# A windowed attention stage: the causal mask written into the score banks by ScalarE, and the value products moved next to the score products

## What is computed

```python
qkv = x @ Wqkv; q, k, v = jnp.split(qkv, 3, -1)          # 16 heads of 64
q = l2norm(q) * qs; k = l2norm(k) * ksc
q = q * cos * scale + rotate_half(q) * sin * scale        # k the same with 1 / scale
# windows of 32 tokens; each window looks at itself and at the one before
bk2, bv2 = (look(bk), look(bv))
mask = (it < jb) | (it > jb + w) | (jb == -1)
sim = jnp.einsum('bhwie,bhwje->bhwij', bq, bk2) * QK_SCALE
sim = jnp.where(mask, -jnp.finfo(sim.dtype).max, sim)
attn = jax.nn.softmax(sim, -1)
out = jnp.einsum('bhwij,bhwje->bhwie', attn, bv2)
x = out @ Wo + x
x = ffn_layer(shift_tokens(x), ...) + x                   # layer norm, W1, gelu gate, W2
```

## Time and profile before

| | before |
|---|---|
| median of three runs | 3678.64 us (3673.33 to 3685.43) |
| span of the profiled execution | 3676.2 us |
| PE busy | 3451.3 us (94%) |
| DVE busy | 2806.8 us (76%) |
| ACT busy | 2365.2 us (64%) |
| POOL busy | 2815.1 us (77%) |
| share of PE in the chain that ended last | 85% |

### The profile page before, as it was taken

How to read it: one execution, slowest core, us unless ns; L and a number is a source line. 1 busy time by engine, 2 the same in 40 slices (tenths; PEclk the granted TensorE clock), 3 DMA queues, 4 the chain that set the end, 5 groups by cost and what they waited for, 6 DMA issues and landing times.

```text
span 3676.2 us, 148973 instructions
## 1 busy us (share of the span) xinstructions
PE 3451.3 (94%) x64612; PEld 2721.5 (74%) x64612; DVE 2806.8 (76%) x4876; ACT 2365.2 (64%) x4307; POOL 2815.1 (77%) x3470
## 2 busy tenths in 40 slices
PE   3799986999999999999999999999999999999997
PEld 2566544788877888777888778877788887788775
DVE  3477666888887888878888878887788888788863
ACT  3333223677766777777777677776677777777663
POOL 1355546998887888878888888888788888888772
PEclk9799997999999999999999999999999999999999
DMA  3333212111111111211111121112111111112110
GB/s 100 98 97 93 87 31 58 47 43 39 46 47 49 40 41 44 51 44 42 45 38 46 44 52 39 42 43 52 40 46 42 40 45 50 44 40 50 36 43 24
DMA packets 126733, 183.48 MB, mean 50 GB/s; under 512 B 29824, under 2 KB 61440, under 8 KB 126080
## 3 DMA queue, kind: packets, MB, share of 16 engines
q1 hardware_dynamic: 119232, 146.15, 15.8%
q0 software_dynamic: 6848, 27.80, 2.5%
HBM read 59.01 MB, written 14.16 MB: 20 GB/s over the span
## 4 chain that ended last, share of the span: by engine, by line
PE 85%; POOL 5%; DVE 3%; issue 3%; ACT 1%; DMA 1%; SPq 0%; ACTq 0%; POOLq 0%; DVEq 0%
PE bank L550 22%; PE bank L622 10%; PE bank L633 9%; PE bank L595 7%; PE bank L560 5%; PE bank L570 4%; PE bank L606 4%; PE bank L696 3%; PE bank L674 3%; PE bank L685 3%; PE bank L582 2%; PE bank L465 1%; PE bank L525 1%; PE bank L642 1%; PE bank L504 1%
## 5 line engine op out<-in xcount | busy, mean ns | idle before, releaser
L550 PE MATMUL bank<-wqkv,xs 128*128 128x512 f32 x3456 | 1061.5, 423 | 17.1 <-DVE m L1029 13.1
L1684 POOL TENSOR_TENSOR m<-m 128x512 f32<-128x512 f32 x576 | 728.7, 1285 | 45.2 <-DVE m L1029 42.6
L550 PEld LDWEIGHTS bank<-wqkv,xs 128*128 128x128 f32 x3456 | 582.8, 191 | 146.0 <-issue 56.9
L1029 DVE TENSOR_TENSOR m<-bank,tab 128x512 f32<-128x512 f32 x768 | 521.5, 679 | 0.7 <-POOL m L1684 0.3
L1358 ACT ACTIVATE sq<-bank 128x512 f32<-128x512 f32 x768 | 458.5, 597 | 98.1 <-PE bank L550 54.2
L1692 POOL TENSOR_TENSOR S<-S,nw 128x1024 f32<-128x1024 f32 x192 | 383.3, 1996 | 168.0 <-DVE S L1060 168.0
L1040 DVE TENSOR_REDUCE ss<-sq 128x8 f32<-128x512 f32 x768 | 504.9, 674 | 0.0
L1700 POOL TENSOR_TENSOR S<-S,rs 128x512 f32<-128x512 f32 x384 | 411.0, 1091 | 69.7 <-DVE rs L1074 67.9
L622 PEld LDWEIGHTS bank<-P,big 64*64 64x64 f32 x24576 | 379.6, 135 | 79.8 <-issue 72.3
L1027 DVE TENSOR_TENSOR m<-bank,tab 128x512 f32<-128x512 f32 x576 | 392.1, 681 | 57.4 <-ACT sq L1358 41.9
L633 PE MATMUL bank<-OT,wo 128*128 128x128 f32 x3072 | 389.9, 282 | 40.8 <-ACT P L1397 27.6
(11 more groups left out here) (232 smaller groups left out, 6457.1 us busy)
## 6 DMA issues: line engine op xcount, KB each, us to landing
big<-vst SPq DMA_DIRECT2D x1536, 64.0 KB
stage<-in_wqkv SPq DMA_DIRECT2D x36, 256.0 KB, 3.0
tab<-in_tab SPq DMA_DIRECT2D x48, 128.0 KB, 2.2
xsort<-big SPq DMA_DIRECT2D x4, 960.0 KB, 8.6
big<-xsort SPq DMA_DIRECT2D x12, 256.0 KB, 4.5
ysort<-big SPq DMA_DIRECT2D x12, 256.0 KB, 3.6
wo<-in_wo SPq DMA_DIRECT2D x6, 512.0 KB, 3.7
big<-in_x SPq DMA_DIRECT2D x8, 256.0 KB, 3.4
```

What stands on the lines that cost most here:

```text
L550: m = eng.matmul(pb[:, :], xt[a], wqkv[:, z, 512 * part:512 * part + 512], start=(n == 0), stop=(n == 2))
L1029: eng.tensor_tensor(m2[:, s3, :].rearrange("p (h s d) -> p h s d", s=2, d=DH // 2), pw, sn.rearrange("p (s d) -> p s d", s=2).unsqueeze(1) ...
L1684: eng.tensor_tensor(turned(g, part), turned(g, part), m2[:, part % 2, :], ALU.add).then_inc(s["g_add"], 1)
```

## The change

TensorE no longer writes the mask. The function mask, its tiles mkb and idb and the five ACT instructions that fill them go. ACT gets masked(g), two copies of 128x512 from the constants kc into the banks 4 and 5, after lessened has read the scores of the round before, and sim waits for a_mk. sim adds onto what ACT has written, with the same flags as before.

values(n - 4) leaves its place between centre and proj(n, 4), and stands directly ahead of sim(n - 2). ACT's out_turned for the half 0 moves from the round's end to the start of the next, next to that for the half 1. The calls masked(n - 2) stand ahead of v_out(n, 0).

```diff
@@ TensorE
-            def mask(g):
-                c = g // 4 % NC
-                pe.wait_ge("a_mb", 5)
-                for par in range(2):
-                    pe.wait_ge("v_sm", 2 * (g - 1) + par + 1)
-                    rows = slice(W * par, W * par + W)
-                    eng.matmul(bank[4 + par][:, :], idb[rows, :], mkb[rows, 0 if c == 0 else 1 + c % 2, :], start=True, stop=False)
...
             def sim(g):
+                pe.wait_ge("a_mk", 2 * g + 2)
...
-                values(n - 4)
                 proj(n, 4)
                 if q4 == 2:
                     up(u - 4, 2)
...
                 turn_k(n - 2, 1)
-                mask(n - 2)
                 proj(n, 5)
                 if q4 == 3:
                     variance(u - 2)
                     end_variance(u - 5)
                 if q4 == 1:
                     gate(u - 4, 2)
+                values(n - 4)
                 sim(n - 2)
@@ ACT
+            def masked(g):
+                c = g // 4 % NC
+                v = KC["mask"].start + 64 * (0 if c == 0 else 1 + c % 2)
+                ac.wait_ge("v_rb", NC)
+                ac.wait_ge("v_tq", NC)
+                for par in range(2):
+                    ac.wait_ge("v_sm", 2 * (g - 1) + par + 1)
+                    eng.activation(bank[4 + par][:, :].rearrange("p (r k) -> p r k", r=8), kc[:, v:v + 64].unsqueeze(1).to_broadcast([P, 8, 64]),
+                                   ACT.Copy, scale=1.0, bias=0.0).then_inc(s["a_mk"], 1)
...
+                out_turned(n - 5, 0)
                 out_turned(n - 5, 1)
...
+                masked(n - 2)
                 v_out(n, 0)
                 square(n, 2)
                 turned_k(n - 2, 0)
                 square(n, 3)
                 turned_k(n - 2, 1)
-                out_turned(n - 4, 0)
                 weights(n, 2)
                 weights(n, 3)
                 v_out(n, 1)
```

More of the change, by code:

```diff
@@ L180, in program @@
         xf = sb("xf", [P, N])
-        mkb = sb("mkb", [2 * W, 3, 512], BF16)
-        idb = sb("idb", [2 * W, P], BF16)
         sq = sb("sq", [P, 2, 512])
@@ L216, in program @@
             p_proj p_tq p_tk p_sim p_pt p_av p_wo p_lnc p_lnv p_lnb p_fg p_fa p_fw p_ec p_ev p_eb
-            a_sq a_vst a_tq a_tk a_exp a_p2 a_oev a_xf a_hi a_halo a_mb a_x2s a_halo2 a_ln a_xn a_xh a_w1 a_gelu a_e a_w
+            a_sq a_vst a_tq a_tk a_exp a_p2 a_oev a_xf a_hi a_halo a_mk a_x2s a_halo2 a_ln a_xn a_xh a_w1 a_gelu a_e a_w
             v_w1 v_xl v_k v_ss v_sm v_max v_sum v_rec2 v_res v_lo v_ln v_xn v_h v_X v_back v_e v_out v_w
@@ L572, in turn_k @@
                 vacant[RING["tk"][h]] = [("a_tk", 2 * g + h + 1)]
-            def mask(g):
-                if not 0 <= g < NG:
-                    return
-                c = g // 4 % NC
-                pe.wait_ge("a_mb", 5)
-                for par in range(2):
-                    pe.wait_ge("v_sm", 2 * (g - 1) + par + 1)
-                    rows = slice(W * par, W * par + W)
-                    eng.matmul(bank[4 + par][:, :], idb[rows, :], mkb[rows, 0 if c == 0 else 1 + c % 2, :], start=True, stop=False)
             def sim(g):
@@ L595, in sim @@
                             m = eng.matmul(bank[4 + par][32 * b:32 * b + 32, 64 * r:64 * r + 64], qT[rows, g % 2, r, 32 * b:32 * b + 32],
-                                           kT[rows, r, :, 4 * i + b, :], start=False, stop=(r == 7))
+                                           kT[rows, r, :, 4 * i + b, :], start=False, stop=(r == 7), skip_group_check=True)
                 m.then_inc(s["p_sim"], 1)
@@ L1263, in _ @@
             ac.wait_ge("d_kc", 32)
[L1264 to L1271, removed]
             for what, c, j in chunk_order("ACT"):
@@ L1384, in turned_k @@
                 eng.activation(d, bank[RING["tk"][h]][:, :].rearrange("p (r t) -> p r t", r=4), ACT.Copy, scale=1.0, bias=0.0).then_inc(s["a_tk"], 1)
+            def masked(g):
+                if not 0 <= g < NG:
+                    return
+                c = g // 4 % NC
[6 more added lines that the diff above has]
+                                   ACT.Copy, scale=1.0, bias=0.0).then_inc(s["a_mk"], 1)
             def exps(g):
@@ L1529, in _ @@
                 v_out(n, 1)
+            out_turned(NG - 3, 0)
             out_turned(NG - 3, 1)
```

## The result

The changed kernel takes 4192.98 us (median of four runs, 4188.52 to 4195.68); the kernel before, run beside it, takes 3675.98 (3672.07 to 3685.43). The ratio is 1.1399, with a 95% interval of 1.138 to 1.1419: 517 us slower. The direction was forecast, the size was not: 3883 was predicted, with 3950 as the upper end.

A forecast was written before the change was run, and what follows sets the result against it. TensorE, without idle time in the four rounds read, was taken as the bound, other engines close behind. Lost cover net of the mask's gain, 187, plus queue, 17, made 204; 3676.2 + 204 + 2.4 = 3883 us, range 3798 to 3950.

The forecast's parts named there:

- Part 3: values(n - 4) moved ahead of sim loses 2 us of cover; 187 us slower, the mask's gain counted.
- part 4: SyncE's copies of vst leave later and delay the loads of wo (8 us) and stage (9 us): 17 in all.
- part 2: ACT's two mask copies a round take 0.5 us each, range 0.5 to 0.65, queued ahead of v_out(n, 0).
- part 1: TensorE loses the two mask products: 0.50 us a round, 96 us over 192 rounds if nothing else becomes late.
- The drain rule: Entering 64-row tiles costs TensorE 0.1 to 0.2 us a round; 19 to 38 us saved, left in the range.
- The clock: Waits of TensorE as short as 2.11 us cost no clock, and the change's waits are 0.3 to 1.4.
- if the granted clock falls in the middle of a layer: One of the signs in the timeline of after that would show the forecast wrong.
- The rival built on it: Waits add up to a granted clock of 0.97, TensorE's work grows 84 us: 3968; chance 0.07.
- the copies landing late: Rival: v_out(n, 0) finds its copies not landed, by 1.5 us in plain rounds and later ones: 3955; chance 0.05.
- Full gain: Rival: ACT and DVE also run 2 us earlier, so the mask's 96 us are had: 3575; chance 0.05.
- cancelling: Rival: stalls of 0.5 a round eat the mask's gain: 3679 plus the queue's 17, or about nothing; chance 0.05.

The follow-up runs named there:

- the run with two wide products: The changed kernel with the 64 value products replaced by two float32 products of 128x512 into the same banks: 3835.03 us, ratio 1.0424.
- the run with the mask alone: Against after, ACT still writes the mask, but the value products and the copy of their first half stand in their old place: 3662.0 us, ratio 0.9954.

## Why the prediction was wrong

**The step that failed is in Part 3: "It costs TensorE the same there".** The sum moved a step of 256 instructions next to another of 256 and carried both at their old durations. Each has its old duration when it runs. What was missing is a term for their instructions: the closest two transfers of 256 start 3.3 us apart, and the two steps together ask for 512 in 3.4. It shows as 225.5 us of waits inside sim. Nothing in the rows that the prediction rests on could show the size of it, but two rows of the profile of before pointed at it. One is in the page's list of queues:

```profile
q8 instruction: 511, 8.37, 1.0%
```

511 pieces of 256 instructions, for 64,612 matmuls and as many weight loads. The other is the wait for issue inside sim, 11 times and 5.9 us in all, shown above: the same wait in its rare form. It was put aside as small, where it should have been asked what makes it rare.

How much it is: the run with two wide products has the order of after without the short instructions and takes 155 us over before. Its stand-in is 0.19 shorter than values in each round, 35 us; with that the change without the supply is about +190. After is +517. The remaining 327 are the supply. The sums by step show where it stands. Each is the time from the start of one of the step's matmuls to the start of the next matmul of any step, over all 192 rounds (from the profiled execution), so that a wait is put down to the step ahead of it:

| us | before | two wide | after |
|---|---|---|---|
| sim | 292 | 307 | 569 |
| proj | 935 | 1052 | 1072 |
| gate | 121 | 190 | 192 |
| turn_k | 173 | 224 | 224 |
| turn_q | 172 | 169 | 199 |
| up | 119 | 136 | 136 |
| mask | 62 | none | none |
| values, or its stand-in | 394 | 358 | 397 |

From before to the run with two wide products the waits for other engines come: proj, gate, turn_k and up. From there to after it is sim, 262 us, and turn_q, 30, which meets the same wait when the count runs out there. proj's 20 fit the lower clock behind the waits, which is argued and not shown. That makes 312 of the 327.

**The cover (part 3) was right.** Medians of the rounds without a border or the load of wo, in us (those of after to 0.2, since the waits for instructions fall unevenly):

| round | before | forecast | two wide, with 0.19 added | after |
|---|---|---|---|---|
| plain | 12.94 | 14.3 | 14.2 | 16.2 |
| gate | 15.07 | 16.4 | 16.3 | 18.1 |
| up | 15.40 | 16.4 | 16.3 | 17.9 |
| centre | 17.20 | 17.6 | 17.7 | 19.5 |

In the third column the terms are +1.2, +1.2, +0.9 and +0.5 where 1.4, 1.3, 1.0 and 0.4 were forecast: with 44 and 48 units as in the prediction about 175 us against 187, and a unit takes 64.5 where 64.7 was forecast. The gate round's stall was to be 1.4, and [1.42 <-ACT gg L1469] stands in the timeline; up 2's 1.0 is [0.89 <-DVE gg L1115]; proj 5 of the plain round does wait for turned_k 0, though only 0.26, since turn_k 1 has already waited 0.71 for v_out ahead of it.

The prediction says of gelu 0 only that it starts after gate 0. In the gate round of the timeline above, most of what lies between the two is one row of ACT:

```profile
2244.39 1.28 ACT L1469 ACT_TABLE_LOAD   x1 [0.94 <-PE bank L663]
```

ACT loads the table for gelu only when gate 0 has ended, though it had been idle for 0.94 us before. Were the load begun in that idle time, gelu 0 could start up to 0.94 earlier here, and the wait of 1.42 would be shorter by as much; this is an estimate, and no run tries it.

**SyncE's queue (part 4) was about right in sum.** What is left of the 190 beside the rounds is 15, against the 17 of the forecast. In the run with two wide products the rounds around the load of wo lie 12 us further over their medians than in before, and those at the borders 8, where 8 and 9 had been taken. TensorE's wait for wo, 2.11 in the earlier trace rows and forecast at 3.8, in after (L622 is out_proj):

```profile
2392.53 3.75 PE L622 MATMUL bank<-OT,wo 128*128 128x128 f32 x16 [3.54 <-issue]
```

Over all five loads it is 17.1 us against 13.2 before, 4 more where 8 were forecast.

**ACT's mask (part 2) was right in its duration.** 0.5 each had been taken:

```profile
2227.27 1.12 ACT L1376 ACTIVATE bank<-kc 128x512 f32<-128x512 f32 x2
2228.33 0.58 ACT L1346 ACTIVATE vst<-bank 128x512 f32<-128x512 f32 x1
```

2228.33 - 2227.27 is 1.06 for two, 0.53 each: nearer to the passes over a bank of the earlier trace rows, 0.50, than to the copy out of SBUF at 0.65. Of the sentence of ScalarE: Activation LUTs of the Trainium skill ("Step-by-step: what each stage is for") that writing PSUM is faster, the trace bears out that much (0.53 against 0.65 for the same kind of source) and no gain over reading a bank.

**The mask's gain (part 1) was right for this change, and not for the mask alone.** In the up round of after, proj 5 starts 2268.26 - 2267.91 = 0.35 after turn_k, where transposes and mask took 0.85, and values follows it after 0.89, where sim followed after 0.90. So the 0.50 is had in full. In the run with the mask alone 36 of the 96 us are given back, since sim or the step before it then waits for turned_k 1. Of the 82 us by which that run missed its expectation these are 36, the waits for issue 32, the 11 that are not accounted for, and 3 by which the kernel before took longer beside it than the 3676 that had been set.

The drain rule from TensorEngine Tiling (Array Packing) of the Trainium skill, "Key Properties", which the prediction left in its range with 19 to 38 us, is no help here: in after the tiles change from 64 by 64 to 64 by 32 between values and sim without a visible gap (2251.37 to 2253.36 is 1.99, the 2.00 of the earlier trace rows), and the 19 to 38 us are small beside the 327 of the supply.

**The clock was wrong in a small way.** "Waits as short as 2.11 cost no clock" doesn't hold: after the wait of 2.27 above, proj at 2238.03 takes 1.63 where it takes 0.94 to 0.97 elsewhere, and the stretch behind that break reads (busy times of PE, PEld, DVE, ACT and POOL, then the granted clock):

```profile
2238.00:2239.70 1.70, 1.70 (x7) 1.30 (x6) 1.47 (x3) 0.76 (x3) 0.15 (x1) 0.50 0.49 116
```

0.50 is the lower level, 1.2 GHz. What went ahead of it was a wait of 2.27 behind three shorter ones (0.33, 0.71, 0.26) in the same round. It was one of the prediction's signs of being wrong, "if the granted clock falls in the middle of a layer". The rival built on it would have given 84 us more on top of the forecast (48 x 1.8 is 86). The clock's whole part is at most 55, an estimate: TensorE was at its lower level for some 190 us of the stack against 81 before, and half of the difference is lost if it had work all that time. 3968 would still have been 225 short.

The other rivals: the copies landing late (3955) show in no row, since v_out has no wait for a DMA, and holding them back until sim has ended leaves the wait as it is. Full gain and cancelling are ruled out by the waits for gelu and hidden, which are there in every kernel that takes values away from proj 4.

## What to carry to other kernels

A step made of many short instructions has a second price beside its time, the number of its instructions, and it is paid by the neighbourhood: before moving one, add up the instructions of what it will stand next to, and compare with what the queue of instructions brings in that time (here 256 in 3.3 us at best). A few waits for issue in the middle of a step that waits for nothing are the first sign, even at 6 us in all; they say that a block of instructions is used up there before the next one is in. Whether they all stand at the same count modulo 256 is a test that one trace is enough for. And when a step leaves its place, ask first what its time covered: the stalls that came out of that question were forecast here to 0.2 us a round.

## What the runs showed of the hardware

TensorE's instructions come in transfers of 16 KB, 256 instructions, and these don't overlap: over the eleven kernels of this study the closest two starts are 3.23 us apart. The transfer of a block starts, in the median of after, 1.1 us after TensorE has entered the block ahead, and TensorE enters the new one 2.15 us after that start at the earliest and 2.5 in the median of the waits. It is a limit in time, not in bytes: at that pace it is 5 GB/s, and in the first of the two views above the queue of instructions is the only one that moves anything.

Runtime: NRT & Kernel Launch of the Trainium skill ("Instruction fetch mechanics") says that the instruction memory is a FIFO refilled in blocks of 16 KiB, 256 instructions, and that the cost of crossing a block is "mostly hidden". The trace agrees on the size of the block. On the second it agrees in the kernel before, with 12.8 us of waits at the boundaries of blocks, and doesn't in the changed one, with 255. The same section gives TensorE a memory of 128 KiB, which would be 2048 instructions; no run here shows such a store, for no transfer starts more than 46 instructions before TensorE enters the block ahead of the one that it brings. What holds the late transfers back stays open, and so does what would let TensorE be refilled earlier.
